# Layer 2's self-attention: three banks take the scores in turn, one takes the results, and ScalarE copies the results out first in an item

## The reference, cut to what matters

```python
qkv = jnp.einsum('bsd,dhf->bshf', x, w_qkv) + b_qkv
q, k, v = jnp.split(qkv, 3, axis=-1)
q = q * cos + _rotate_half(q) * sin
k = k * cos + _rotate_half(k) * sin
scores = jnp.einsum('bhqd,bhkd->bhqk', q, k) / jnp.sqrt(jnp.float32(f))
scores = scores + alibi[None]
scores = jnp.where(causal == 0, -1000000000.0, scores)
weights = jax.nn.softmax(scores, axis=-1)
attn = jnp.einsum('bhqk,bhkd->bhqd', weights, v).transpose(0, 2, 1, 3)
return jnp.einsum('bshd,hdm->bsm', attn, w_out) + b_out
```

## Time and profile before

| | us |
|---|---|
| three runs | 2618.58, 2601.89, 2617.25 |
| median | 2617.25 |
| the profiled execution | 2606.97 |
| its span | 2605.2 |
| PE busy | 2128.2 (82%) |
| DVE busy | 1592.5 (61%) |
| ACT busy | 1141.6 (44%) |
| POOL busy | 723.5 (28%) |
| the stage of the change | about 1205 to 1651 |

### The profile page before, as it was taken

One profiled execution on the slowest core, in us unless ns is written; L12 is line 12 of the kernel. 1 busy time (PEld: TensorE's weight loads), 2 busy tenths in 40 slices (PEclk: granted clock), 3 DMA queues, 4 the chain that ended last, 5 costly groups with the idle time before them and its releaser, 6 DMA issues. The chain is left out here.

```text
span 2605.2 us, 36929 instructions
## 1 busy us (share of the span) xinstructions
PE 2128.2 (82%) x12720; PEld 1296.7 (50%) x12720; DVE 1592.5 (61%) x3752; ACT 1141.6 (44%) x2176; POOL 723.5 (28%) x909
## 2 busy tenths in 40 slices
PE   7784996767748888997888988785998896778898
PEld 4573672225612324664444544472343565567567
DVE  4677347988848883455555554453566447466686
ACT  2443427654436663224766766432445322133310
POOL 0330004644331100003555655334443000243000
PEclk8796897998959998998999999885799897788895
DMA  1100000001042100003323331103220001000000
GB/s 37 37 1 6 1 1 6 1 7 47 1 116 48 42 1 1 1 1 103 81 71 79 80 82 45 50 1 67 52 49 2 1 1 68 28 1 1 1 1 17
DMA packets 38601, 80.35 MB, mean 31 GB/s; under 512 B 7344, under 2 KB 21680, under 8 KB 37392
## 3 DMA queue, kind: packets, MB, share of 16 engines
q1 hardware_dynamic: 35952, 75.00, 10.9%
q10 hardware_dynamic: 2464, 2.99, 0.4%
HBM read 51.75 MB, written 7.34 MB: 23 GB/s over the span
## 5 line engine op out<-in xcount | busy, mean ns | idle before, releaser
L740 ACT ACTIVATE spt<-P 128x1024 f32<-128x1024 f32 (+3 forms) x256 | 221.0, 863 | 185.8 <-PE P L594 185.8
L707 DVE TENSOR_REDUCE smf<-P 128x2 f32<-128x1024 f32 (+3 forms) x256 | 254.3, 1019 | 48.5 <-PE P L583 25.2
L2238 PEld LDWEIGHTS P<-W,e_h 128*128 128x128 f32 (+1 forms) x1952 | 241.3, 206 | 50.7 <-issue 41.2
L2381 DVE SCALAR_TENSOR_TENSOR X<-P,WE,X 128x128 f32<-128x128 f32 x576 | 162.1, 344 | 147.7 <-PE P L2238 144.3
L2238 PE MATMUL P<-W,e_h 128*128 128x128 f32 (+1 forms) x1952 | 248.7, 294 | 2.4 <-DVE X L2381 1.3
L1094 POOL TENSOR_TENSOR d_e<-d_e,d_rc 128x512 f32<-128x512 f32 (+3 forms) x256 | 180.1, 725 | 176.8 <-DVE d_rc L1000 146.8
L2224 PE MATMUL P<-XT,W 128*128 128x512 f32 x424 | 220.3, 617 | 1.5 <-PEq L230 1.5
L2265 ACT ACTIVATE e_g<-P 128x512 f32<-128x512 f32 x148 | 88.4, 597 | 278.3 <-PE P L2224 273.9
L1043 ACT ACTIVATE d_e<-d_e,d_mn 128x512 f32<-128x512 f32 (+3 forms) x256 | 141.7, 554 | 132.2 <-DVE d_mn L992 131.8
L2281 DVE TENSOR_TENSOR e_h<-e_g,P 128x512 f32<-128x512 f32 x148 | 101.1, 684 | 92.5 <-PE P L2228 92.4
L2228 PE MATMUL P<-XT,W 128*128 128x512 f32 x296 | 155.6, 608 | 1.6 <-DVE e_h L2281 1.5
(11 more groups left out here) (388 smaller groups left out, 4133.3 us busy)
## 6 DMA issues: line engine op xcount, KB each, us to landing
d_bt<-in_alibi SPq DMA_DIRECT2D x32, 512.0 KB, 3.7
d_moved<-d_raw SPq DMA_DIRECT2D x256, 64.0 KB, 2.4
ska<-parts_k SPq DMA_DIRECT2D x72, 64.0 KB
sqa<-parts_q SPq DMA_DIRECT2D x72, 64.0 KB
W<-in_w_L_xattn SPq DMA_DIRECT2D x1, 4291.0 KB, 13.7
W<-in_w_L_ffn SPq DMA_DIRECT2D x1, 3333.0 KB, 11.0
W<-in_w_L_ffn SPq DMA_DIRECT2D x1, 3155.0 KB, 10.2
parts_k<-sparts SPq DMA_DIRECT2D x8, 384.0 KB, 2.5
```

The lines of the kernel that those rows point to most:

```text
L707: v.tensor_reduce(MF[:, n % 2, u, :], P[:, bank:bank + 2, 0:wide(u)], AX.X, ALU.max, negate=True).then_inc(s("max"), 1)
L740: a.activation(PT[:, n % 3, :, t, N - late(t):N], P[:, BANK_T:BANK_T + 2, 0:late(t)], ACT.Exp, scale=SC).then_inc(s("exp"), 1)
L2238: last = pe.matmul(P[:, PY + j % 2, 128 * t:128 * (t + 1)], HT[rows, q % RING, blk, 128 * t:128 * (t + 1)], w2, start=n == 0, stop=n == le ...
L2381: last = v.scalar_tensor_tensor(x, y, k.WE[:, 4 * c + t, e:e + 1], x, ALU.mult, ALU.add)
```

## The change

The scores get three banks (0, 1 and 5), taken in turn by a running count of pieces over heads, steps and items. `scores` now waits for one reduction less (count 2(4n+j) - 1 in place of 2(4n+j)): of the step before, only the first head's reduction has to be done. Bank 5 is taken from the results: all items accumulate in bank 4, so w0 of an item waits until ACT has copied out the item just before (`o_out` of n, where it was n - 1). And in ACT's order `outputs` stands ahead of `raw` at the start of a turn.

```diff
-    BANK_S, BANK_T, BANK_O, BANK_Y, BANK_P = 0, 2, 4, 6, 7
+    BANKS_S, BANK_T, BANK_O, BANK_Y, BANK_P = (0, 1, 5), 2, 4, 6, 7
...
+        def scored(n, j, h):
+            return P[:, BANKS_S[(2 * (QT * n + j) + h) % 3], :]
...
             def scores(n, j):
                 u = QT - 1 - j
                 pe.wait_ge(s("roped"), 2 * n + 2)
-                pe.wait_ge(s("biased"), 2 * (QT * n + j))
+                if n or j:
+                    pe.wait_ge(s("biased"), 2 * (QT * n + j) - 1)
                 wd = 128 * (u + 1)
                 for h in range(2):
                     r = slice(64 * h, 64 * h + 64)
-                    last = pe.matmul(P[:, BANK_S + h, 0:wd], QR[r, n % 2, 128 * u:128 * (u + 1)], KR[r, n % 2, 0:wd], start=True, stop=True)
+                    last = pe.matmul(scored(n, j, h)[:, 0:wd], QR[r, n % 2, 128 * u:128 * (u + 1)], KR[r, n % 2, 0:wd], start=True, stop=True)
                 last.then_inc(s("score"), 1)
 
             def weighted(n, t):
                 if t == 0:
                     pe.wait_ge(s("t_out"), 2 * QT * (n + 1))
-                    if n >= 2:
-                        pe.wait_ge(s("o_out"), n - 1)
+                    pe.wait_ge(s("o_out"), n)
                 for h in range(2):
                     r = slice(64 * h, 64 * h + 64)
-                    last = pe.matmul(P[r, BANK_O + n % 2, 128 * t:N], VP[:, n % 3, t, r], PT[:, n % 2, h, t, 128 * t:N],
+                    last = pe.matmul(P[r, BANK_O, 128 * t:N], VP[:, n % 3, t, r], PT[:, n % 2, h, t, 128 * t:N],
                                      start=t == 0, stop=t == QT - 1)
...
                 for h in range(2):
-                    v.tensor_tensor_reduce(piece(n, h, u), P[:, BANK_S + h, 0:wd], BT[:, n % 4, h, N - wd:N], -SC, 3e38,
+                    v.tensor_tensor_reduce(piece(n, h, u), scored(n, j, h)[:, 0:wd], BT[:, n % 4, h, N - wd:N], -SC, 3e38,
                                            ALU.add, ALU.min, MN[:, n % 2, u, h:h + 1]).then_inc(s("biased"), 1)
...
-                a.activation(OT[:, n % 2, :], P[:, BANK_O + n % 2, :], ACT.Copy).then_inc(s("o_out"), 1)
+                a.activation(OT[:, n % 2, :], P[:, BANK_O, :], ACT.Copy).then_inc(s("o_out"), 1)
 
             w_ready(a)
             for n in range(ITEMS + 6):
                 for j in range(QT):
+                    if j == 0 and 0 <= n - 5 < ITEMS:
+                        outputs(n - 5)
                     if j % 2 == 0 and n < ITEMS:
                         raw(n, j // 2)
-                    if j == 0 and 0 <= n - 5 < ITEMS:
-                        outputs(n - 5)
```

## The result

| | before | changed |
|---|---|---|
| median of 22 runs, us | 2611.36 | 2620.89 |
| profiled execution, us | 2606.97 | 2617.28 |
| its span, us | 2605.2 | 2615.4 |
| ratio of the times | 1 | 1.0041 (95% interval 1.0023 to 1.0058) |
| one item in the middle of the stage, us | 13.53 | 13.93 |

What follows compares the result with a forecast made beforehand. A loop through several engines, PE its longest part, was taken as the bound at 13.53 us per item. Terms summed to +10.9 us: 2617.9 from the profiled execution, 2628.2 from the median; middle 2623, range 2608 to 2640.

Steps and rivals of the forecast that it cites:

- The new loop: s1, last exponentials, ACT's copy of the results, w0, next s1: 13.94 us per item against 13.53, +0.41.
- The swap at no cost: ACT's order, outputs ahead of raw: raw comes 0.47 us later, hidden by w0 and s0, cost 0.
- The sum: Whole execution, all terms added: -1.0 + 9.4 + 1.6 - 0.3 + 0.6 + 0.6 = +10.9 us.
- the terms for the turns from 5 on: Later turns, w0 waiting for the results' copy: +9.4, +1.6, -0.3, +0.6 and +0.6 us.
- The turn with the second `add`: One of three turns where `add` on DVE delays the last exponentials: +0.52 us each, +1.6 together.
- turns 2 to 4: Early turns with earlier scores and no w0 that waits: -0.33 us each, -1.0 together.
- The clock: Rival: PE's added idle time makes low-clock stretches more frequent; one in each second item gives +36 us, 2653; chance 0.05.
- The relief "alone -0.33": s3 waits only for the first reduction of step 2 and starts earlier: -0.33 us per item by itself.
- the first rival: Earlier s3 kept, w0's wait covered: 30 x -0.33 = -10 us, 2607; chance 0.05.
- The floor of 12.06: PE's item time without its gaps of 0.83 before s3 and 0.64 before t3: 12.06 us.
- w0's gap: PE's new wait before w0 for ACT's copy of the results: 0.74 us.

Runs made afterwards that it cites:

- both waits back: Changed kernel, but the scores wait again for both reductions of the step before: 13.93 us per item, ratio 1.0064.
- Two experiments: by_cos and by_sin behind step 2's reductions, on the changed kernel with early results copy; by_cos behind step 2, by_sin behind step 3, on the kernel before: both 12.71 us.
- a third at 12.75: Kernel before with by_cos and by_sin of j = 2 behind the reductions of step 2 on DVE: 12.75 us per item, ratio 0.9892.
- the fastest version: Kernel before with by_cos behind step 2, by_sin behind step 3 on DVE, and the transposes' copy ahead of raw at j = 2: 12.41 us, ratio 0.9854.

## Why the prediction was right, and where it was not

**The new loop: right.** 13.94 was forecast, 13.93 came, and its parts with it: the copy and hop, that is, from ACT's end to PE's start (0.73; 0.72 measured), the last exponentials not moved by an earlier s3 (7.76 after s1; 7.75 measured), the loss passed on whole from w0 to the next s1. The copy's place enters the item in full (14.50 with `raw` first), and with the copy out of the way the loss is gone (13.34). At another pace the same sum gave 13.29 and 13.29 came, so the hundredths were not luck.

**The swap at no cost: right**, shown alone (13.53) and by DVE's remaining wait of 0.35 for s0.

**The sum: right in the stage, in part by luck over the whole.** +10.9 was forecast for the profiled execution, 2617.28 - 2606.97 = +10.3 measured; the medians differ by 9.5. From the first w0 (in turn 4) to the last one it is 413.51 before and 425.81 changed, +12.3, where the terms for the turns from 5 on add up to +11.9. The turn with the second `add`, together with the one before it, grew from 27.78 to 28.73, so 0.95 for 0.52 + 0.41. All that lies outside these turns was 2.1 shorter in the changed execution. The prediction has 1.0 of that, for turns 2 to 4, and this is not shown: s3 of turn 3 does wait 0.34 less, but from the first s0 to the first w0 the changed kernel took 26.35 at a granted clock of 0.75, against 24.45 at 0.86 before. The predicted time, 2623, was halfway between sums on 2606.97 and on a median of three runs that was 5.9 us above that of 22. That this halfway base, 2612.1, met the median of 22, 2611.36, was luck.

**The clock: it did not fall.** The granted clock of the changed kernel is 0.879 over the whole execution (0.878 before). These are its stretch to set beside the earlier trace rows, and its one item of the middle below 1.00:

```profile
1300.00:1350.00 50.00, 45.50 (x266) 24.50 (x264) 23.58 (x84) 33.83 (x99) 28.24 (x36) 1.00 0.29 77
1356.22:1371.37 15.15, 13.89 (x73) 7.62 (x73) 7.05 (x25) 9.94 (x29) 8.02 (x10) 0.89 0.32 88
```

The kernel before has one such item too, of 15.17 at 0.89. The rule of the Trainium skill that the rival named (TensorE: Matmul & The Clock Gate, A second HAM failure mode) did not come to bear on gaps of at most 0.64 us, 1.87 us in all per item. One profile stands apart: with both waits back, five items ahead of the last turns ran at 0.89 to 0.96, with no more idle time per item. The profiles of five other kernels show no such item at all. What sets off these dips stays open.

**The relief "alone -0.33": mis-sized.** The step computed its worth from the loop through s3 and went no further. Measured alone it was 0.15 (13.38), and 0.19 with the next loop opened (13.34). By the distance of items the first rival, priced at 0.33 for each of 30 items, was therefore at most about -6 us and not -10. The forecast did not suffer, since the relief was buried under w0's wait anyhow, but the rival's number was wrong.

**The floor of 12.06: wrong as a bound for less waiting.** I took PE's gaps as 0.83 and 0.64 that could vanish each by itself. The 0.64 before t3 belongs to a loop through s1 of 12.70. Two experiments stopped there, at 12.71, where 12.1 to 12.4 was expected from the same floor, and a third at 12.75 a little above. And w0's gap was forecast as 0.74 and came as 0.61, because t0 in front of it had started to wait, by 0.13, for the copies of step 3: the prediction let t0 come 0.33 earlier without looking at what t0 waits for.

Over the item of the kernel before lies, then, a stack of loops over the same engines. Their lengths, as the experiments laid them bare one by one: through s3 13.53, through t1 13.38, through t0 13.34, through t3 12.70, and PE's own work 12.06 (this last one is a sum of rows; no kernel reached it). The change lowered the first to about 13.20, a sum of rows too, since the loops through t1 and t0 hide it, and put a new one of 13.93 on top.

The rule on rotating banks (the Trainium skill, Perfetto Trace Analysis, Optimizing Tensor Performance) agrees with the traces for the results' bank, whose rotation hid 0.40 us per item. For the scores a third place was worth 0 in the change, and 0.15 to 0.19 where no other loop stood above it.

What stays open: whether the relief by a third bank pays in the fastest version, where s3 waits 0.28 again; it was not run.

## What to carry to other kernels

In a pipeline of engines that runs at a fixed distance per item, follow every wait back until it reaches itself, and write down all such loops with their lengths, not only the longest: a saving is worth the distance to the second longest, and a new wait costs the distance by which its loop exceeds the longest. When a buffer's double is given up, the price is set by where its reader stands in its engine's order: against the 13.53 of before, the kernel with a single results bank took 0.97 us per item more with the copy second, 0.40 more with the copy first, and 0.19 less with the copy before the last exponentials, where the relief of the scores shows at last. Before moving buffers, look at the order of work on the engine waited for: reordering VectorE and ScalarE, with all banks as before, gave 1.5%. No arrangement of banks tried here reached that without DVE's new order; the best gave 0.5%, with ScalarE reordered too.

## What the runs showed of the hardware

The rotary products on VectorE (128x512, f32) take 0.68 to 0.69 us in the rows of the middle of the stage where GpSimd is quiet, and mostly 1.00 to 1.14 where GpSimd's products run beside them. The `by_cos` of the changed kernel starts 0.48 us later behind the last exponentials and is 0.37 shorter, 0.69 for 1.06. But the loss does not always fall on VectorE: with late rotary products in the kernel before, the `by_cos` at 1421.97 took 0.69 beside two GpSimd products of 128x256, and these took 1.71 together where they took 1.19 in the kernel before. The reductions that read scores from PSUM (128x512) stay at 0.66 to 0.69 beside GpSimd's products. No run here isolates what the two engines share.

A matmul that waits for ScalarE's copy of the transposes or of the results, or for VectorE's reductions, started 0.14 to 0.16 us after their end in every kernel of the series where the view shows that wait, steady enough to add up loops to 0.01 us. `projected`, which waits for the copy of the values, started only 0.05 to 0.06 after it (the kernels with the copies of step 0 first on ACT); why it is less there is not shown.
